# Mixing four experts of each tile in one accumulator on VectorE, with three PSUM banks for their outputs

## The reference

```python
def _L0_ffn_ref(x, router_w, router_b, expert_w, expert_b):
    E, K = 8, 2
    router_probs = softmax(x @ router_w + router_b)
    top_p, top_i = top_k(router_probs, K)
    top_p = top_p / sum(top_p)
    expert_out = einsum('bnd,edc->bnec', x, expert_w) + expert_b
    gathered = take_along_axis(expert_out, top_i[..., None], axis=2)
    return einsum('bnk,bnkc->bnc', top_p, gathered)
...
t = t + _L0_ffn_ref(_ln_t(t), ...)       # t: 100352 tokens of 128 features
```

## Time and profile before

| | |
|---|---|
| median of 3 runs | 8317.02 us (8311.66 to 8319.39) |
| the profiled execution's own time | 8316.43 us |
| its span, first to last instruction | 8314.5 us |
| busy over the span: PE / DVE / ACT / POOL | 92% / 74% / 58% / 72% |
| expert stage, first to last expert matmul | 1882.1 to 3720.6 us |

### The profile page before, as it was taken

One profiled execution on the slowest core, in us unless ns is written; L12 is line 12 of the kernel. 1 busy time (PEld: TensorE's weight loads), 2 busy tenths in 40 slices (PEclk: granted clock), 3 DMA queues, 4 the chain that ended last, 5 costly groups with the idle time before them and its releaser, 6 DMA issues. The chain is left out here.

```text
span 8314.5 us, 428968 instructions
## 1 busy us (share of the span) xinstructions
PE 7686.1 (92%) x164847; PEld 4672.0 (56%) x164847; DVE 6157.6 (74%) x20999; ACT 4825.9 (58%) x15717; POOL 5973.0 (72%) x7343
## 2 busy tenths in 40 slices
PE   7999999978999999988979999979999799999999
PEld 6777777764444444436753333327777555555555
DVE  7999999979999999988856777758888322222222
ACT  4666666655566565558975555536666444444444
POOL 7888888868888888878966666637777444444444
PEclk9999999999999999999999999989999899999999
DMA  1222222222333333317885666658988122222222
GB/s 51 58 57 59 58 57 58 58 59 79 100 107 107 101 108 107 101 59 245 305 266 149 161 165 163 164 136 226 236 228 224 53 58 58 58 58 58 58 58 53
DMA packets 836450, 948.54 MB, mean 114 GB/s; under 512 B 329994, under 2 KB 701067, under 8 KB 812812
## 3 DMA queue, kind: packets, MB, share of 16 engines
q1 hardware_dynamic: 835404, 942.12, 40.4%
q10 hardware_dynamic: 576, 1.84, 0.1%
HBM read 574.02 MB, written 445.22 MB: 123 GB/s over the span
## 5 line engine op out<-in xcount | busy, mean ns | idle before, releaser
L988 PE MATMUL moe_pe_out<-moe_we,moe_xnT 128*128 128x512 f32 x3136 | 1474.9, 604 | 150.8 <-DVE moe_acc L882 143.6
L2329 ACT ACTIVATE rec_yT<-rec_ph 128x16 f32<-128x16 f32 x6272 | 871.9, 184 | 944.1 <-PE rec_ph L2462 939.8
L784 ACT ACTIVATE moe_scaled<-moe_pe_out,moe_gate 128x128 f32<-128x128 f32 x3136 | 894.4, 368 | 652.5 <-PE moe_pe_out L988 650.5
L2462 PEld LDWEIGHTS rec_ph<-rec_yT,rec_vt 128*32 128x32 f32 x50160 | 792.7, 108 | 690.3 <-ACT rec_yT L2329 585.1
L2462 PE MATMUL rec_ph<-rec_yT,rec_vt 128*32 128x16 f32 x50160 | 1087.6, 192 | 16.4 <-issue 6.3
L988 PEld LDWEIGHTS moe_pe_out<-moe_we,moe_xnT 128*128 128x128 f32 x3136 | 543.1, 190 | 912.2 <-issue 911.1
L2376 DVE COPY rec_xT<-rec_pin 128x512 f32<-128x512 f32 x196 | 135.6, 692 | 1212.9 <-PE rec_pin L2423 1212.9
L1622 PE MATMUL conv_p<-conv_c,conv_toep 32*32 32x432 f32 (+3 forms) x20480 | 960.8, 532 | 9.2 <-DVE conv_out L1587 4.7
L307 POOL TENSOR_SCALAR att_xn<-att_xin,att_mv,att_rstd 128x128 f32<-128x128 f32 x1024 | 868.1, 858 | 54.1 <-POOL att_rstd L303 54.1
L722 POOL TENSOR_TENSOR moe_paired<-moe_scaled 128x256 f32<-128x256 f32 x784 | 583.4, 744 | 162.3 <-ACT moe_scaled L784 123.0
L2304 POOL TENSOR_SCALAR rec_xn<-rec_xin,rec_mv,rec_rstd 128x127 f32<-128x127 f32 x784 | 634.7, 823 | 41.5 <-POOL rec_rstd L2301 41.5
(11 more groups left out here) (210 smaller groups left out, 19679.7 us busy)
## 6 DMA issues: line engine op xcount, KB each, us to landing
c<-foc_cs SPq DMA_DIRECT2D x128, 448.0 KB, 7.9
conv_cin<-c SPq DMA_DIRECT2D x64, 896.0 KB, 7.2
att_xin<-x_windows SPq DMA_DIRECT2D x512, 98.0 KB
moe_xin<-x SPq DMA_DIRECT2D x112, 448.0 KB, 6.4
x<-moe_acc SPq DMA_DIRECT2D x112, 448.0 KB, 2.8
foc_xin<-x SPq DMA_DIRECT2D x32, 1568.0 KB, 8.2
q<-foc_qs SPq DMA_DIRECT2D x32, 1568.0 KB, 8.4
ctx_all<-conv_out SPq DMA_DIRECT2D x128, 392.0 KB
```

What stands on the lines that cost most here:

```text
L784: ins = act.activation(scaled[:, b, e, :], pe_out[:, b, 1, e * C:(e + 1) * C], ACT.Identity, scale=g)
L988: pe.matmul(pe_out[:, b, half, :], xnT[:, n.slot(2), t, :], we[:, half * 4:half * 4 + 4, :].rearrange("d e c -> d (e c)"), start=True, sto ...
L2329: act.activation(yT[:, a, column(t, half)], ph[:, a, half, sums(t)], ACT.Sigmoid).then_inc(moved[half], 1)
L2462: ins = pe.matmul(ph[r:r + 32, n.slot(2), half, sums(t)], vt[:, r:r + 32], before, start=False, stop=True, skip_group_check=True)
```

## The change

The second accumulator `odd` and the instruction `add_odd` go. All four experts of a tile are added in `acc` in that tile's turn; the order becomes expert 0 (with the token), expert 1, `add_others` of the tile before, expert 2, expert 3. Each of the three later experts waits by a `hold` for the expert before it. There are five places for routing instructions instead of six, so k = 7 moves from the last place of tile 2 to the second of tile 3, and the last instruction stays in tile 4. Experts 0 to 3 get three PSUM banks instead of two (experts 4 to 7 keep two), so TensorE's product for them waits for VectorE's tile t - 3. TensorE's loop goes over 12 groups, so that a tile's bank is a constant. The load of a later group waits for `begun`, which counts experts 0 and 1, in place of `mixing`.

```diff
+    U_PE = 12
+    DVE_BANKS = 3
...
-        odd = S.sb("odd", [P, 2, C])
...
-        pe_out = S.ps("pe_out", [P, 2, 2, BANK])
+        pe_act = S.ps("pe_act", [P, 2, BANK])
+        pe_dve = S.ps("pe_dve", [P, DVE_BANKS, BANK])
...
-        MIX = 4
+        MIX = 2
...
-                        hold(sp, mixing, n.val(T * MIX), ticks)
+                        hold(sp, begun, n.val(T * MIX), ticks)
...
-                k = 6 * (t - 1) + place - 4
+                k = 5 * (t - 1) + place - 4
...
+            def expert_0(n, t, first):
                 if t == 0:
                     hold(dve, routing, n.val(ROUTE_OPS, ROUTE_OPS), ticks)
                 if t == 0 and first >= 4:
                     hold(dve, x2_out[n.slot(4)], n.turn(4, 16), ticks)
+                dve.wait_ge(expert_done[0], n.val(T, t + 1))
+                gated(n, t, 0, xin[:, n.slot(4), t, :]).then_inc(begun, 1)
+
+            def expert_1(n, t):
+                hold(dve, begun, n.val(T * MIX, MIX * t + 1), ticks)
+                gated(n, t, 1).then_inc(begun, 1)
+
+            def expert_2(n, t):
+                hold(dve, begun, n.val(T * MIX, MIX * t + 2), ticks)
+                gated(n, t, 2).then_inc(mixing, 1)
+
+            def expert_3(n, t):
+                hold(dve, mixing, n.val(T * MIX, MIX * t + 1), ticks)
+                gated(n, t, 3).then_inc(mixing, 1)
+
+            def add_others(n, t):
+                b = (n.off * T + t) % 2
+                a = acc[:, n.slot(4), t, :]
+                hold(dve, mixing, n.val(T * MIX, MIX * t + 2), ticks)
+                dve.wait_ge(others_ready, n.val(T, t + 1))
+                dve.tensor_tensor(a, a, others[:, b, :], ALU.add).then_inc(mixed, 1)
+
+            def mix(n, t, first, more):
+                expert_0(n, t, first)
+                route_between(n, t, 0, more)
+                expert_1(n, t)
                 route_between(n, t, 1, more)
                 if first >= 1 or t >= 1:
-                    add_odd(n, t - 1)
+                    add_others(*tile_of(n, t, 1))
                 route_between(n, t, 2, more)
+                expert_2(n, t)
                 route_between(n, t, 3, more)
+                expert_3(n, t)
                 route_between(n, t, 4, more)
...
-            def add_odd(n, t):
-                a, b = tile_of(n, t)
-                hold(dve, mixing, n.val(T * MIX, MIX * (t + 1)), ticks)
-                dve.tensor_tensor(a, a, odd[:, b, :], ALU.add).then_inc(joined, 1)
...
+                k = n.off * T + t
+                for half, out in ((1, pe_act[:, k % 2, :]), (0, pe_dve[:, k % DVE_BANKS, :])):
+                    if half and (first >= 1 or t >= 2):
+                        hold(pe, scaled_ready, n.val(T, t - 1), ticks)
+                    if not half and (first >= 1 or t >= DVE_BANKS):
+                        hold(pe, mixing, n.val(T * MIX, MIX * (t - DVE_BANKS + 1)), ticks)
+                    pe.matmul(out, xnT[:, n.slot(2), t, :],
...
-            run_steps(pe, N, U, step, 4)
+            run_steps(pe, N, U_PE, step, 4)
```

More of the change, by code:

```diff
@@ L639, in expert_stage @@
         expert_done = S.sems("expert_done", 2)
-        mixing, joined, mixed = S.sem("mixing"), S.sem("joined"), S.sem("mixed")
+        begun, mixing, mixed = S.sem("begun"), S.sem("mixing"), S.sem("mixed")
         scaled_ready, paired_ready, others_ready = S.sem("scaled_ready"), S.sem("paired_ready"), S.sem("others_ready")
@@ L783, in pick @@
                     g = gate[:, n.slot(2), t, 4 + e:5 + e]
-                    ins = act.activation(scaled[:, b, e, :], pe_out[:, b, 1, e * C:(e + 1) * C], ACT.Identity, scale=g)
+                    ins = act.activation(scaled[:, b, e, :], pe_act[:, b, e * C:(e + 1) * C], ACT.Identity, scale=g)
                 ins.then_inc(scaled_ready, 1)
@@ L870, in route_between, with tile_of, gated @@
             def route_between(n, t, place, more):
-                k = 6 * (t - 1) + place - 4
+                k = 5 * (t - 1) + place - 4
                 if more and 0 <= k < ROUTE_OPS:
                     route(n + 1, k)
-            def gated(n, t, e, into, start=False, onto=None):
+            def tile_of(n, t, back):
+                m, u = (n, t - back) if t >= back else (n - 1, t - back + T)
+                return m, u
+            def gated(n, t, e, onto=None):
                 g = gate[:, n.slot(2), t, e:e + 1]
[L878 to L890, removed]
+                src = pe_dve[:, (n.off * T + t) % DVE_BANKS, e * C:(e + 1) * C]
+                into = acc[:, n.slot(4), t, :]
+                return dve.scalar_tensor_tensor(out=into, in0=src, scalar=g, in1=into if onto is None else onto,
+                                                op0=ALU.mult, op1=ALU.add)
@@ L891, in mix @@
+            def expert_0(n, t, first):
                 if t == 0:
                     hold(dve, routing, n.val(ROUTE_OPS, ROUTE_OPS), ticks)
-                dve.wait_ge(expert_done[0], n.val(T, t + 1))
-                gated(n, t, 1, odd[:, b, :], start=True)
-                route_between(n, t, 0, more)
                 if t == 0 and first >= 4:
                     hold(dve, x2_out[n.slot(4)], n.turn(4, 16), ticks)
-                gated(n, t, 0, acc[:, n.slot(4), t, :], onto=xin[:, n.slot(4), t, :])
+                dve.wait_ge(expert_done[0], n.val(T, t + 1))
+                gated(n, t, 0, xin[:, n.slot(4), t, :]).then_inc(begun, 1)
@@ L899, in mix @@
+            def mix(n, t, first, more):
+                expert_0(n, t, first)
+                route_between(n, t, 0, more)
+                expert_1(n, t)
                 route_between(n, t, 1, more)
                 if first >= 1 or t >= 1:
-                    add_odd(n, t - 1)
+                    add_others(*tile_of(n, t, 1))
                 route_between(n, t, 2, more)
-                hold(dve, mixing, n.val(T * MIX, MIX * t + 1), ticks)
-                gated(n, t, 3, odd[:, b, :])
+                expert_2(n, t)
@@ L905, in mix @@
                 route_between(n, t, 3, more)
-                if first >= 1 or t >= 1:
-                    add_others(n, t - 1)
+                expert_3(n, t)
                 route_between(n, t, 4, more)
[L909 to L916, removed]
@@ L950, in step @@
                 if not more:
-                    add_odd(n, T - 1)
                     add_others(n, T - 1)
```

## The result

The changed kernel takes 8897.8 us (median of 4 runs, 8885.5 to 8906.8) against 8317.2 before: a ratio of 1.0697, 95% interval 1.0683 to 1.071. The forecast was 8286 us, range 8210 to 8358. The profiled execution took 8906.8 us, its span is 8905.0.

The account below looks back on a forecast made before the run. DVE was taken to bound the expert stage, 16.36 us a group. 14.04 - 1.40 + 2.44 + 1.0 of port waits = 16.08, 0.28 less, times 112: 31 us off 8317, so 8286 us, range 8210 to 8358.

Parts of the forecast that it names:

- the one on the third bank and the loop: Expert stage, PE: its group without its wait is 15.12 us, below 16.08, so PE doesn't set the time.
- my rivals: Expert stage: slower, chance 0.30; same within 0.2%, chance 0.18; dependence nearly free, chance 0.05.
- The sum for the expert stage: DVE's group in the expert stage: 15.08 + 1.0 = 16.08 us, 0.28 less than now, times 112: 31 us.
- The walk through GpSimd's group: Expert stage: follows POOL's work against DVE's tiles to see which additions meet a `pair`; sum 0.8 us a group.
- port waits: DVE additions of two SBUF operands waiting until POOL's addition ends; forecast 1.0 us a group after the change.
- The dependent slot: DVE, expert stage: an expert reading its predecessor's result starts 0.48 us behind it, against 0.26 now; lower bound 0.37.
- 15.08 without port waits: DVE's group in the expert stage: 14.04 - 1.40 for removed `add_odd` + 2.44 for dependence = 15.08 us.
- Waits outrun the addition: Slower rival, expert stage: port waits keep their present rate, 16.6 us a group, +28 us, 8345; chance 0.30.
- The dependence costs little: Rival, expert stage: experts follow as if independent, PE's 15.12 us sets the group, 139 us less, 8178; chance 0.05.
- What costs nothing: Expert stage: later `pair` of tile 4, third bank, loop of 12, POOL's sum and SP's load add no time.

Follow-up runs that it names:

- e1: Kernel before, with 71 idle semaphore increments in TensorE's stream ahead of the last stage and nothing else: 8899.2 us, ratio 1.0667.
- e2: Changed kernel with 185 idle semaphore increments in TensorE's stream ahead of the third stage: 8312.7 us, ratio 0.9992.
- e4: Kernel before with only TensorE's loop over 12 groups, both accumulators and two banks kept: 8868.0 us, ratio 1.0635.
- e3: Changed kernel with two banks and TensorE's loop over 4 groups, so one accumulator alone: 8298.6 us, ratio 0.9967.
- e7: One accumulator, two banks, TensorE's loop of 4, plus 30 idle increments on VectorE at the third stage's start: 8290.8 us, ratio 0.9938.
- e6: One accumulator, two banks, TensorE's loop of 4, plain waits instead of holds between a tile's experts: 8242.7 us, ratio 0.9887.
- e8: Changed kernel, three banks, with TensorE's loop over 6 groups in place of 12: 8301.7 us, ratio 0.9965.
- e9: One accumulator, plain waits, three banks for experts 0 to 3, TensorE's loop over 6 groups: 8237.6 us, ratio 0.9903.
- e12: Kernel before with 226 idle semaphore increments on VectorE at the start of the third stage: 8342.1 us, ratio 1.002.

## Why the prediction was wrong

**The step that failed** is the one on the third bank and the loop: "so it doesn't set the time, at any loop length; its loop of 12 branches less often, and no row separates that." I costed the loop of 12 inside its own stage only, where it is indeed harmless. It makes TensorE's stream longer, and that moved the recurrence's loop from a counted start of 76, where it stays loaded, to 147, where it is fetched again in 45 of 94 passes. That cost 597 us, against a range whose upper end was 41 us above no change. e1, e2 and e4 show it from three sides. None of my rivals reached outside the expert stage.

**The sum for the expert stage held.** Forecast 0.28 us a group and 31 us; measured 27 us in the stage, and a group of 16.0 us in the median and 16.2 in the mean against 16.08 forecast; 24 us with the accumulator alone (e3). The same with VectorE's place in the third stage put back (e7) is 29 us below the kernel before measured alongside. The walk through GpSimd's group chose between 0.8 and 1.63 us of port waits, and no run separates its single meetings, so that the sum came out within 4 us is in part luck.

**The dependent slot** was 0.48 us as taken from rows 9, and 0.37 with plain waits, the lower bound of rows 10. By the Trainium skill's rule (VectorE: DVE Perf Modes, on the drain) a semaphore between chained instructions costs nothing extra. It doesn't hold for these dependent experts: with the plain wait they start 0.37 us behind their predecessor, where independent ones take 0.26. The other 0.11 us is the instruction that `hold` adds, and worth 49 us in the expert stage.

**Port waits:** forecast 1.0 us a group in all. `add_others` alone fell from 0.98 to 7 x 0.057 = 0.4. What is left of the group above the forecast's 15.08 without port waits is 0.9 us in the median and 1.1 in the mean, and it was not split further. "Waits outrun the addition" did not happen. That GpSimd's `pow` and its normalising don't hold up an addition was right: in the changed kernel the 99 additions that lie within `pow` take 282 ns in the median and the 304 within the normalising 301, against 497 for the 100 within a `pair`.

**"The dependence costs little"** did not happen: the slot was 0.48 us. Where e6 made the dependence cheaper, the group came down, but to 15.8 and not to PE's 15.1, since port waits came back and 0.11 us of the dependence stayed.

**What costs nothing:** the third bank, right as a gain of nothing (e8 against e3, e9 against e6). The later place of `gap` makes ScalarE wait 2.9 us a group instead of 0.6, and PE 1.2 us for ScalarE's bank; no run shows a loss of time by it.

**Not foreseen besides:** the third stage's 11 us, from VectorE's place (e7, e12), and the convolution's 8, one pass fetched again.

**Open:** why only some passes fetch again between 110 and 201, two at 110 and all 94 at 201, and why the convolution's loop, at 172 and 173, had one such pass the first time and none the other; both places would touch eight blocks with a start 36 to 45 behind the count. Open too is what in the third stage waits, and how the port waits of the other instructions changed.

## What to carry to other kernels

Unrolling is paid outside its stage as well: whoever changes the length of an instruction stream should compare every stage, and the packets of the instruction queues, before believing a total. For TensorE's loops of 1637 and 1586 instructions the place decides, and some idle instructions ahead of it, or a smaller unrolling elsewhere, move it out of the bad places. By the same count of blocks it would decide from about 1540 instructions on; that is an estimate, and no run tests it. A chain of dependent instructions should wait by the plain form: the extra sequencer instruction costs 0.11 us a time where the wait is real. In the kernel before, instructions behind a `hold` with nothing to wait for kept slots of 0.20 and 0.26 us. Here some 8320 us became 8243 by one accumulator and plain waits; the third bank and the loop of 12 were not needed.

## What the runs showed of the hardware that was not expected

TensorE fetches its instructions in packets of 16.4 KB, 256 instructions, one every 3.8 us when it must fetch in a row (the changed kernel's recurrence). The loop of 1637 instructions takes 18.1 us a pass when it stays loaded and 31 to 32 when it is fetched. Nineteen instructions of place can decide: at a counted start of 201 the stage takes 3130 us, at 220 it takes 1818. The granted clock in the changed kernel's recurrence is 0.88 where it was 0.99; it is 0.50 from 6572 to 6582 us, after PE had stood still from 6570.2 on.

GpSimd's additions of 128x128 and 128x256 hold up VectorE's additions of two SBUF operands; its `pow` on 128x7 and its normalising don't (282 and 301 ns against 497 within a `pair`).
